# Rounding in ScalarE's affine step, 16-bit transposes of the low halves, and two buffers for two tiles

## The chip, the cores and the metric

The kernel runs on one core of a Trainium2 chip. The metric is the device time of one execution in microseconds (us): the median of three runs of the kernel before is 655.27 us (654.14 to 655.77).

## The reference, cut to what matters

The input `x` is 64 samples of 64 channels by 1024 positions, fp32. Two layers run one after the other:

```python
y  = grouped_conv1d(x, w, taps=9, groups=4) + ctx(cond)[:, :, None] + bias   # L0_cond
# L0_ffn: int8 quantised product
a_scale = max(abs(y), -1) / 127 ; x_q = round(y / a_scale)
w_scale = max(abs(W0), -1) / 127 ; w_q = round(W0 / w_scale)
x  = x + ((x_q @ w_q.T) * a_scale * w_scale).astype(float16)
# L1_cond: a 64x64 mix of the channels per sample, from a small network with softmax
x2 = einsum('boi,bih->boh', agg_w, x) + agg_b[:, :, None]
# L1_ffn: x2 @ W.T + b, plus a rank-32 term gated by a top-2 softmax over 8 experts
x  = x + H + delta
```

## The kernel before, in words

A tile is two samples, that is 128 rows (2 x 64 channels) by 1024 positions; there are NT = 32 tiles. Each engine has its own program, written out by hand, and works it off in order; semaphores (`wait(engine, name, value)` and `.then_inc`) join them. Nothing is planned by a compiler: the order in the text is the order on the engine.

**Before the loop** (about 50 us): the 1024x1024 weight of the first layer is loaded in 8 blocks of 128 rows. VectorE takes each row's maximum (`wq_maxima`), its scale and inverse, and rounds (`wq_round`): times the inverse plus MAGIC. MAGIC is 1.5 x 2^23, so that the fp32 sum has the rounded integer in its low bits. TensorE transposes the blocks as fp32 (`wq_transposed(o, h)`, L421, four 128x128 pieces for each half h into one PSUM bank), and ScalarE writes them as bf16 into `wqT` with bias -MAGIC (`wq_out`, L822). Between these stand the first tiles' steps and the mixing weights: `agg_out` (L831) writes them to `zT`, SyncE stores them to DRAM (L285), loads them back as `mixT` (L290), and then goes on with the loads of the loop, among them `x_ph` for tile 4 and `wst` (L312).

**The loop**, c from 3 to 31. TensorE's order in iteration c is: `conv(c)` (L452), `mix(c-3)` (L495), logits, the first half of `int_product(c-2)` (L511) with `row_total(c-3)` (L475) behind its third matmul, the second half with `max_rows(c)` (L518) inside, `max_back(c)` (L522), `tokens_out(c-1)` (L483), and in odd iterations `rank_pair(c-5)` (L542, L545). The second half of `conv(c)`'s groups waits for `f_ready` of `layer0(c-2, 1)`.

VectorE's order is: `rank_out` in even iterations, `rounded(c-1)` (L1274), `conv_bias(c)` (L1246), `row_max(c)` (L1252), `tile_bound` and `tile_scale` (L1288 to L1295, they give `t_up`), `layer0(c-2, 0)` (L1284), `chan_max(c)`, `low(c-3, 0)` (L1300), `scales(c)` (its last operation gives `yinv`, L1269), `layer0(c-2, 1)`, `low(c-3, 1)`.

ScalarE's order is: `tokens_sb(c-2)` (L845), `row_sums(c-3)` (L840, it gives `x1sum`), `w_abs` in iterations 3 to 10 (L868, from `wst`), `w_high` in 13 to 20 (L878), `w_sums` in 19 to 26 (L873), `high(c-3)` twice (L855), `z_bias` in 4 to 7 (L920), and `scale_rows(c)` (L862).

The path of the tokens of tile t is: `conv_bias` writes `yb` (fp32); `scale_rows` multiplies each of 8 slices by its own inverse scale into `yv` (fp32); `rounded` adds MAGIC and takes it off again, and writes `yq` (bf16); `tokens_out` transposes 8 pieces into PSUM; `tokens_sb` copies them as bf16 into `yqT`; `int_product` multiplies with `wqT`. There is one buffer each of `yb`, `yv`, `yq` and `yqT`. So `conv_bias(t)` waits for `scale_rows(t-1)` (`yv_ready`), and `tokens_sb(t)` for the whole of `int_product(t-1)`. GpSimd adds the residual (`add_layer0`, L1090) and splits weights.

**After the loop** TensorE runs the dense product of the second layer (L574), then 13 pairs of tiles with 7 products each in place of 8 (L768), and the rank term (L750).

## Time and profile before

| | |
|---|---|
| median of three runs | 655.27 us |
| profiled execution: its time | 654.78 us |
| its span, first to last instruction | 653.0 us |
| mean granted clock of TensorE | 0.987 of full speed |
| TensorE busy | 631.6 us (97%) |
| VectorE busy | 435.8 us (67%) |
| ScalarE busy | 337.1 us (52%) |
| GpSimd busy | 336.6 us (52%) |
| share of the chain that ended last | TensorE 75% |

A busy share is an average over stages. The matmuls are pipelined, so a busy TensorE is not one at its peak. "Idle before <-X" in a row is the time for which the engine stood still just before that instruction, and what ended it. In the profile PE is TensorE, PEld its weight loads, DVE VectorE, ACT ScalarE, POOL GpSimd, SP SyncE.

### The profile page before, as it was taken

The page shows a single profiled execution, that of the slowest core. Times are in us where ns is not written, and L with a number is a line of the kernel's source. Part 1 is how long each engine was busy: PE and PEld are TensorE (multiplying, and loading weights), DVE is VectorE, ACT ScalarE, POOL GpSimd, SP SyncE. Part 2 cuts the span into 40 slices and gives each one's busy share as a digit, 9 for nine tenths or more (in the row PEclk, how much of TensorE's full clock was granted, in tenths as well). Part 3 has the DMA queues.
Part 4 walks back from the last instruction along what each step waited for, and adds up shares of the span by engine and source line. Part 5 has one row for each costly group of instructions (what it writes and reads, how often), then busy time and mean ns, then how long its engine had stood idle before and what let it go on. Part 6 is the DMA issues. An engine that isn't in the chain of part 4 may idle for free.

```text
span 653.0 us, 14999 instructions
## 1 busy us (share of the span) xinstructions
PE 631.6 (97%) x5853; PEld 340.6 (52%) x5886; DVE 435.8 (67%) x922; ACT 337.1 (52%) x574; POOL 336.6 (52%) x222
## 2 busy tenths in 40 slices
PE   6998999999999999999999999999999999999997
PEld 4565555556665666665554444444444444444443
DVE  5866887888888888889636697746544333444434
...
GB/s 271 330 132 312 299 296 302 203 243 319 266 288 337 313 347 299 260 213 179 194 132 291 97 34 122 181 222 188 194 193 187 145 123 132 187 194 247 75 1 129
DMA packets 46628, 138.39 MB, mean 212 GB/s; under 512 B 13156, under 2 KB 13444, under 8 KB 46377
## 3 DMA queue, kind: packets, MB, share of 16 engines
...
q14 instruction: 23, 0.19, 0.1%
...
## 4 chain that ended last, share of the span: by engine, by line
PE 75%; DVE 1%; issue 1%; ACT 0%; DVEq 0%; ACTq 0%
PE ps L768 36%; PE ps L511 11%; PE ps L574 9%; PE ps L452 8%; PE ps L495 3%; PE ps L750 2%; PE ps L483 2%; PE ps L542 1%; PE ps L545 1%; PE ps L557 1%; PE ps L522 0%; PE ps L518 0%; ACT yv L862 0%; DVE unscale L1452 0%; DVE z_lo L1311 0%
## 5 line engine op out<-in xcount | busy, mean ns | idle before, releaser
L1090 POOL TENSOR_TENSOR x<-x_in,f_both 128x512 f32<-128x512 f32 x64 | 74.1, 1159 | 201.6 <-DVE f_both L1284 201.6
L511 PE MATMUL ps<-wqT,yq_both 128*128 128x512 bf16 x479 | 113.7, 379 | 6.7 <-issue 4.3
L452 PE MATMUL ps<-x_ph,conv_w 64*64 64x256 f32 (+1 forms) x1024 | 97.2, 392 | 1.6 <-DMA conv_w<-in_conv_taps 1.6
L862 ACT ACTIVATE yv<-yb,yinv 128x128 f32<-128x128 f32 x256 | 78.2, 388 | 26.5 <-DVE yinv L1269 26.3
L901 ACT ACTIVATE ring<-ring,ratio 128x2048 f16<-128x2048 f16 x26 | 50.6, 1994 | 51.0 <-DVE x_ph L1548 14.0
L768 PE MATMUL ps<-ffn_wT,ring 128*128 128x512 f16 x312 | 71.6, 379 | 0.0
L511 PEld LDWEIGHTS ps<-wqT,yq_both 128*128 128x128 bf16 x512 | 45.2, 97 | 49.1 <-ACT yq_both L845 1.5
L452 PEld LDWEIGHTS ps<-x_ph,conv_w 64*64 64x64 f32 (+1 forms) x1024 | 51.1, 137 | 36.6 <-issue 14.4
L855 ACT ACTIVATE ring<-ps,t_up 128x512 f16<-128x512 f32 x64 | 40.5, 684 | 47.0 <-issue 39.4
L574 PE MATMUL ps<-ffn_wT,ring 128*128 128x512 f16 x288 | 64.6, 379 | 0.0
L1121 POOL TENSOR_TENSOR bias_b<-ring 128x1024 f32<-128x1024 f16 x13 | 27.8, 2137 | 48.3 <-ACT ring L901 48.2
L1561 DVE SCALAR_TENSOR_TENSOR x_in<-ps,unscale,x_in 128x512 f32<-128x512 f32 x30 | 22.5, 750 | 43.7 <-PE ps L768 43.5
L1284 DVE SCALAR_TENSOR_TENSOR f_both<-ps,tok_scale,wsc_b 128x512 f16<-128x512 f32 x64 | 47.7, 747 | 4.0 <-PE ps L511 3.9
L768 PEld LDWEIGHTS ps<-ffn_wT,ring 128*128 128x128 f16 x312 | 30.5, 98 | 36.8
L1300 DVE SCALAR_TENSOR_TENSOR ring<-ps,t_up,ring 128x512 f16<-128x512 f32 x64 | 46.9, 736 | 0.8 <-ACT ring L855 0.8
L1246 DVE TENSOR_TENSOR yb<-ps,ybias 128x1024 f32<-128x1024 f32 x32 | 39.0, 1220 | 11.7 <-PE ps L452 8.8
L1561 DVE SCALAR_TENSOR_TENSOR wst<-ps,unscale,wst 128x512 f32<-128x512 f32 x28 | 21.0, 749 | 35.2 <-PE ps L768 35.1
L574 PEld LDWEIGHTS ps<-ffn_wT,ring 128*128 128x128 f16 x288 | 27.2, 98 | 31.8 <-issue 0.8
L1252 DVE TENSOR_REDUCE rowmax<-yb 128x8 f32<-128x1024 f32 x32 | 39.0, 1220 | 1.0
L495 PEld LDWEIGHTS ps<-mixT,x 64*64 64x64 f32 x2048 | 35.5, 135 | 5.0 <-issue 1.3
L1561 DVE SCALAR_TENSOR_TENSOR x<-ps,unscale,x 128x512 f32<-128x512 f32 x21 | 15.8, 750 | 31.1 <-PE ps L768 31.1
L1274 DVE TENSOR_SCALAR yq_both<-yv 128x1024 bf16<-128x1024 f32 x32 | 23.4, 731 | 18.5 <-ACT yv L862 18.5
...
## 6 DMA issues: line engine op xcount, KB each, us to landing
...
```

The source lines that it names most:

```text
L452: return mm(ps_conv[o, g * 2 * MB:(g + 1) * 2 * MB], conv_w[k, g, w.start + o.start:w.start + o.stop], xp[k, g, :, view], start=first, sto ...
L495: last = mm(bank(2 + e)[j * 64:(j + 1) * 64, k * CH:(k + 1) * CH], x1[b, t % 2, l:l + 64], mixT[b, t, b], start=True, stop=True)
L511: last = mm(acc_bank(t, h), yqT[:, p, :], wqT[:, p, h * HALF:(h + 1) * HALF], start=p == 0, stop=p == PH - 1)
L574: last = mm(o, x2_cols[:, x2_slot(n), a, k, :], ffn_wT[:, w, k, h * HALF:(h + 1) * HALF], start=k == 0 and i == 0, stop=k == NL - 1 and i ...
L768: last = mm(b, left(a, k), right(w, k), start=fresh and k == 0 and i == 0, stop=k == 3 and i == 2, skip_group_check=True)
L855: A(x2_cols[:, t % RING, 0, :, h * CH:(h + 1) * CH], bank(2 + h).rearrange("p (c t) -> p c t", c=NL), ACT.Copy, scale=t_up[:, t % 4:t % 4 ...
L862: last = A(yv[:, s, :], yb[:, s, :], ACT.Copy, scale=yinv[:, s:s + 1])
L901: A(cols, cols, ACT.Copy, scale=ratio[:, t:t + 1]).then_inc(sem("norm_ready"), 1)
L1090: g.tensor_tensor(x1[:, t % 2, s], x_in[:, t % 3, s], f16[:, s], ALU.add).then_inc(sem("x1_ready"), 1)
L1284: v.scalar_tensor_tensor(f16[:, s], acc_bank(t, h), tok_scale[:, t % 4:t % 4 + 1], wsc_b[:, s], ALU.mult, ALU.mult).then_inc(sem("f_ready" ...
L1300: v.scalar_tensor_tensor(x2_cols[:, t % RING, 1, :, cols], bank(2 + h).rearrange("p (k t) -> p k t", k=NL), t_up[:, t % 4:t % 4 + 1], x2_c ...
L1561: v.scalar_tensor_tensor(buf, src, unscale[:, t:t + 1], buf, ALU.mult, ALU.add).then_inc(sem("pair_folded"), 1)
```

## The change

- MAGIC grows by 0x6600. The low 16 bits of the fp32 sum are then 0x6600 plus the integer, which read as fp16 is 1536 plus the integer, exactly.
- `scale_rows` adds MAGIC itself: Copy with a scale becomes Identity with a scale and a bias, both read per partition. `rounded` and its buffer are gone; `yq` is a view of `yv`, every second fp16.
- `tokens_out` and `wq_transposed` transpose these fp16 low halves (8 pieces of a weight block into one bank, one eviction); `tokens_sb` and `wq_out` take 1536 off by their bias.
- `yb` and `yqT` have two buffers each; `conv_bias(t)` waits for `scale_rows(t-2)` and `tokens_sb(t)` for `int_product(t-2)`.
- ScalarE runs `tokens_sb(c-1)` in iteration c ahead of `scale_rows(c)`. It ran it in iteration c+1 ahead of `row_sums`.
- `row_total` stands behind the fourth matmul, not the third, and `tokens_out(31)` between the halves of `int_product(30)`.

```diff
--- before.py
+++ after.py
@@ -31,7 +31,8 @@
 NJ = NANCH // P
 ZW = 64 + ZR
 QMAX = 127.0
-MAGIC = 12582912.0
+HALF_BIAS = 1536.0
+MAGIC = 12582912.0 + 0x6600
 EXPMASK = 0x7F800000
 TOP = 13
 RING = 6
@@ -84,11 +85,11 @@
         agg = zT[:, 0:CH * 32].rearrange("b (i o) -> b i o", i=CH)
         x_in = sb("x_in", [P, 3, L], F32)
         x_ph = sb("x_ph", [P, 3, GRP * 2 * MW], F32)
-        yb = sb("yb", [P, 8, MB], F32)
+        yb = sb("yb", [P, 2, 8, MB], F32)
         yv = sb("yv", [P, 8, MB], F32)
         yq_both = sb("yq_both", [P, 2, L], BF16)
-        yq = yq_both[:, 0, :].rearrange("p (s m) -> p s m", s=8)
-        yqT = yq_both[:, 1, :].rearrange("p (s m) -> p s m", s=PH)
+        yq = yv[:, :, :].bitcast(F16).rearrange("p s (m w) -> p s m w", w=2)[:, :, :, 0]
+        yqT = yq_both[:, :, :].rearrange("p a (s m) -> p a s m", s=PH)
         f_both = sb("f_both", [P, 2, L], F16)
         f16 = f_both[:, 0, :]
         abs_junk = f_both[:, 1, :].bitcast(BF16)
@@ -101,6 +102,7 @@
         b_rank = row_bias[0:R, :]
         ident = sb("ident", [P, P], F32)
         identb = sb("identb", [P, P], BF16)
+        identh = sb("identh", [P, P], F16)
         ones16 = sb("ones16", [P, 1], F16)
         ones_b = sb("ones_b", [P, P], BF16)
         conv_w = sb("conv_w", [P, GRP, 16 * CG], F32)
@@ -121,7 +123,8 @@
         att_s = sb("att_s", [B, 4], F32)
         attT = sb("attT", [NK, B], F32)
         set_mask = sb("set_mask", [P, 8], F32)
-        neg_magic = sb("neg_magic", [P, 1], F32)
+        magic = sb("magic", [P, 1], F32)
+        neg_half_bias = sb("neg_half_bias", [P, 1], F32)
         wq_max = sb("wq_max", [P, NL], F32)
         wq_scale = sb("wq_scale", [P, NL], F32)
         wq_inv = sb("wq_inv", [P, NL], F32)
@@ -171,7 +174,7 @@
         gmx = sb("gmx", [P, 8], F32)
         g_top = sb("g_top", [2, 1], F32)
 
-        gate = yb[:, :, :].rearrange("p n (j e) -> p n j e", e=E)
+        gate = yb[:, 0, :, :].rearrange("p n (j e) -> p n j e", e=E)
         top8 = yv[:, 0, :].rearrange("p (j e) -> p j e", e=E)
         gateT = wsc_b[:, 0:P]
 
@@ -181,7 +184,7 @@
             return ps[:, n * 512:(n + k) * 512]
 
         ps_conv, ps_mix, ps_tr, ps_small, ps_dense = bank(0, 2), bank(2, 2), bank(4), bank(5), bank(6, 2)
-        ps_trb = ps_tr.bitcast(BF16)
+        ps_trh = ps_tr.bitcast(F16)
         ps_g = bank(2, 4)
 
         agg_dram = nc.dram_tensor("agg_scratch", [2, B, CH, 32], F32, kind="Internal").ap()
@@ -412,13 +415,14 @@
         def _(pe):
             mm, tr = nc.tensor.matmul, nc.tensor.transpose
 
-            def wq_transposed(o, h):
+            def wq_transposed(o):
                 pe.wait_ge(sem("wq_rounded"), o + 1)
-                if o >= 1:
-                    pe.wait_ge(sem("wqT_ready"), 2 * o - 1 + h)
-                q = wq_nat[:, o * L:(o + 1) * L].rearrange("p (m e) -> p e m", e=PH)
-                for p in range(4):
-                    last = tr(bank(6 + h)[:, p * P:(p + 1) * P], q[:, 4 * h + p, :], ident[:, :])
+                if o == 0:
+                    pe.wait_ge(sem("ident_ready"), 3)
+                wait(pe, "wqT_ready", o - 1)
+                q = wq_nat[:, o * L:(o + 1) * L].bitcast(F16).rearrange("p (m e w) -> p e m w", e=PH, w=2)
+                for e in range(PH):
+                    last = tr(bank(6 + o % 2).bitcast(F16)[:, e * P:(e + 1) * P], q[:, e, :, 0], identh[:, :])
                 last.then_inc(sem("wqT_psum"), 1)
 
             def wq_scales_out(h):
@@ -475,12 +479,12 @@
                 mm(ps_small[:, 140:141], ones_b[:, :], top, start=True, stop=True).then_inc(sem("total_psum"), 1)
 
             def tokens_out(t):
-                wait(pe, "yq_ready", t + 1)
+                wait(pe, "yv_ready", t + 1)
                 wait(pe, "yqT_ready", t)
                 if t == 0:
                     pe.wait_ge(sem("agg_ready"), 4)
                 for s in range(8):
-                    last = tr(ps_trb[:, s * P:(s + 1) * P], yq[:, s, :], identb[:, :])
+                    last = tr(ps_trh[:, s * P:(s + 1) * P], yq[:, s, :], identh[:, :])
                 last.then_inc(sem("yqT_psum"), 1)
 
             def mix(t):
@@ -501,14 +505,14 @@
                     wait(pe, "yqT_ready", t + 1)
                     wait(pe, "f_ready", 2 * t - 1 + h)
                     if t == 0:
-                        pe.wait_ge(sem("wqT_ready"), 8 * h + 8)
+                        pe.wait_ge(sem("wqT_ready"), 4 * h + 4)
                         pe.wait_ge(sem("wsc_ready"), h + 1)
                     elif h == 1:
                         wait(pe, "yb_ready", min(t + 3, NT))
                     if t >= NT - 2:
                         pe.wait_ge(sem("yb_ready"), NT)
                 for p in range(lo, hi):
-                    last = mm(acc_bank(t, h), yqT[:, p, :], wqT[:, p, h * HALF:(h + 1) * HALF], start=p == 0, stop=p == PH - 1)
+                    last = mm(acc_bank(t, h), yqT[:, t % 2, p, :], wqT[:, p, h * HALF:(h + 1) * HALF], start=p == 0, stop=p == PH - 1)
                 if hi == PH:
                     last.then_inc(sem("acc_ready"), 1)
 
@@ -594,40 +598,32 @@
-            wq_transposed(0, 0)
-            wq_transposed(0, 1)
+            wq_transposed(0)
...
@@ -659,9 +655,9 @@
                     wait(pe, "yinv_ready", c)
                     for j in logits_at[c]:
                         logits_out(j)
-                int_product(c - 2, 0, 0, 3)
+                int_product(c - 2, 0, 0, 4)
                 row_total(c - 3)
-                int_product(c - 2, 0, 3, 8)
+                int_product(c - 2, 0, 4, 8)
                 int_product(c - 2, 1, 0, 3)
                 if c == W_BOUND + 1:
                     pe.wait_ge(sem("w_scale_ready"), 2)
@@ -688,8 +684,8 @@
             dense(0, 0, 4, 8)
             row_total(NT - 3)
             int_product(NT - 2, 0)
+            tokens_out(NT - 1)
             int_product(NT - 2, 1)
-            tokens_out(NT - 1)
             dense(0, 1, 0, 5)
             mix(NT - 2)
             int_product(NT - 1, 0)
@@ -817,10 +813,9 @@
             A = nc.scalar.activation
 
             def wq_out(o):
-                for h in range(2):
-                    act.wait_ge(sem("wqT_psum"), 2 * o + h + 1)
-                    A(wqT[:, 4 * h:4 * h + 4, o * P:(o + 1) * P], bank(6 + h).rearrange("p (e c) -> p e c", e=4),
-                      ACT.Identity, bias=neg_magic[:, 0:1]).then_inc(sem("wqT_ready"), 1)
+                act.wait_ge(sem("wqT_psum"), o + 1)
+                A(wqT[:, :, o * P:(o + 1) * P], bank(6 + o % 2).bitcast(F16).rearrange("p (e c) -> p e c", e=PH),
+                  ACT.Identity, bias=neg_half_bias[:, 0:1]).then_inc(sem("wqT_ready"), 1)
 
             def wsc_out(h):
                 act.wait_ge(sem("wsc_psum"), h + 1)
@@ -841,9 +836,9 @@
 
             def tokens_sb(t):
                 wait(act, "yqT_psum", t + 1)
-                wait(act, "acc_ready", 2 * t)
-                A(yqT[:, :, :].rearrange("m p (s c) -> m s p c", s=8),
-                  ps_trb.rearrange("m (s p c) -> m s p c", s=8, p=PH), ACT.Copy).then_inc(sem("yqT_ready"), 1)
+                wait(act, "acc_ready", 2 * (t - 1))
+                A(yqT[:, t % 2, :, :].rearrange("m p (s c) -> m s p c", s=8),
+                  ps_trh.rearrange("m (s p c) -> m s p c", s=8, p=PH), ACT.Identity, bias=neg_half_bias[:, 0:1]).then_inc(sem("yqT_ready"), 1)
 
             def high(t, h):
                 wait(act, "mix_ready", 2 * t + 1 + h)
@@ -857,9 +852,9 @@
 
             def scale_rows(t):
                 wait(act, "yinv_ready", t + 1)
-                wait(act, "yq_ready", t)
+                wait(act, "yqT_psum", t)
                 for s in range(8):
-                    last = A(yv[:, s, :], yb[:, s, :], ACT.Copy, scale=yinv[:, s:s + 1])
+                    last = A(yv[:, s, :], yb[:, t % 2, s, :], ACT.Identity, scale=yinv[:, s:s + 1], bias=magic[:, 0:1])
                 last.then_inc(sem("yv_ready"), 1)
 
             def w_abs(k):
@@ -926,7 +921,7 @@
             A(h1[:, :], bank(2)[:, 64:64 + B], ACT.Gelu, bias=mb01[:, 1:2]).then_inc(sem("h_act"), 1)
             act.wait_ge(sem("att_logits_ready"), 2)
             A(att_e[:, :], att[:, :], ACT.Exp, bias=att_s[:, 0:1]).then_inc(sem("att_exp_ready"), 1)
-            act.wait_ge(sem("ident_ready"), 3)
+            act.wait_ge(sem("ident_ready"), 5)
             wq_out(0)
             act.wait_ge(sem("mlp_psum"), 4)
             A(attT[:, :], bank(2)[0:NK, 192:192 + B], ACT.Copy).then_inc(sem("attT_ready"), 1)
@@ -960,8 +955,6 @@
             A(z_w[:, :, R:ZR], pk[:, PACK["w8"]].rearrange("p (k r) -> p k r", k=NL), ACT.Copy, scale=s_up[:, 0:1]).then_inc(sem("rank_hi_ready"), 1)
 
             for c in range(3, NT):
-                if c > 3:
-                    tokens_sb(c - 2)
                 row_sums(c - 3)
                 if 0 <= c - W_ABS < NL:
                     w_abs(c - W_ABS)
@@ -982,9 +975,9 @@
                     act.wait_ge(sem("b_loaded"), 16)
                     for n in (0, 2):
                         A(b_parts[n * R:(n + 1) * R, :], b_rank, ACT.Copy, scale=s_up[0:R, 3:4]).then_inc(sem("rank_hi_ready"), 1)
+                tokens_sb(c - 1)
                 scale_rows(c)
 
-            tokens_sb(NT - 2)
             t_high(0)
             row_sums(NT - 3)
             high(NT - 3, 0)
@@ -1061,11 +1054,13 @@
             g = nc.gpsimd
             g.memset(ident[:, :], 0.0).then_inc(sem("ident_zero"), 1)
             g.memset(identb[:, :], 0.0).then_inc(sem("ident_zero"), 1)
-            pool.wait_ge(sem("ident_zero"), 2)
-            for m in (ident, identb):
+            g.memset(identh[:, :], 0.0).then_inc(sem("ident_zero"), 1)
+            pool.wait_ge(sem("ident_zero"), 3)
+            for m in (ident, identb, identh):
                 g.affine_select(out=m[:, :], in_=m[:, :], compare_op=ALU.not_equal, fill=1.0, base=0,
                                 pattern=[[-1, P]], channel_multiplier=1).then_inc(sem("ident_ready"), 1)
-            g.memset(neg_magic[:, :], -MAGIC).then_inc(sem("ident_ready"), 1)
+            g.memset(neg_half_bias[:, :], -HALF_BIAS).then_inc(sem("ident_ready"), 1)
+            g.memset(magic[:, :], MAGIC).then_inc(sem("ident_ready"), 1)
 
             def mixT_zero(e):
                 g.memset(mixT[e * CH:(e + 1) * CH, :, (1 - e) * CH:(2 - e) * CH], 0.0).then_inc(sem("mixT_zeroed"), 1)
@@ -1242,14 +1237,14 @@
 
             def conv_bias(t):
                 wait(dve, "conv_ready", t + 1)
-                wait(dve, "yv_ready", t)
-                v.tensor_tensor(yb[:, :, :].rearrange("p (b g) m -> p b g m", b=2), ps_conv.rearrange("p (g b m) -> p b g m", g=GRP, b=2),
+                wait(dve, "yv_ready", t - 1)
+                v.tensor_tensor(yb[:, t % 2, :, :].rearrange("p (b g) m -> p b g m", b=2), ps_conv.rearrange("p (g b m) -> p b g m", g=GRP, b=2),
                                 ybias[:, 2 * t:2 * t + 2, :].unsqueeze(3).to_broadcast([P, 2, GRP, MB]), ALU.add).then_inc(sem("yb_ready"), 1)
 
             def row_max(t):
                 wait(dve, "yb_ready", t + 1)
                 wait(dve, "rowmaxT_ready", t)
-                v.tensor_reduce(rowmax[:, :], yb[:, :, :], AX.X, ALU.max, apply_absolute_value=True).then_inc(sem("rowmax_ready"), 1)
+                v.tensor_reduce(rowmax[:, :], yb[:, t % 2, :, :], AX.X, ALU.max, apply_absolute_value=True).then_inc(sem("rowmax_ready"), 1)
 
             def chan_max(t):
                 wait(dve, "rowmaxT_ready", t + 1)
@@ -1267,12 +1262,6 @@
                 wait(dve, "tok_scale_ready", t + 1)
                 wait(dve, "yv_ready", t)
                 v.reciprocal(yinv[:, :], yscale[:, :]).then_inc(sem("yinv_ready"), 1)
-
-            def rounded(t):
-                wait(dve, "yv_ready", t + 1)
-                wait(dve, "yqT_psum", t)
-                v.tensor_scalar(yq[:, :, :].rearrange("p s m -> p (s m)"), yv[:, :, :].rearrange("p s m -> p (s m)"), MAGIC, -MAGIC,
-                                ALU.add, ALU.add).then_inc(sem("yq_ready"), 1)
 
             def layer0(t, h):
                 wait(dve, "acc_ready", 2 * t + h + 1)
@@ -1376,7 +1365,6 @@
-            rounded(0)
...
@@ -1433,7 +1419,6 @@
                     v.tensor_reduce(w_max[:, :], w_part[:, :], AX.X, ALU.max).then_inc(sem("w_max_ready"), 1)
 
             rank_out(NT - 6)
-            rounded(NT - 1)
             row_scales()
             for t in (NT - 3, NT - 2):
                 tile_bound(t)
```

## Rows read from the trace of the kernel before

**Rows 1.** Busy time by engine in two stretches: stretch, length, busy us (instructions) per engine.

```profile
60.00:100.00 40.00, 38.57 (x585) 24.08 (x592) 33.06 (x82) 35.88 (x75) 10.45 (x9) 1.00 0.80 297
...
209.60:227.70 18.10, 17.78 (x265) 11.13 (x264) 15.78 (x39) 14.55 (x32) 14.55 (x9) 1.00 0.91 336
```

**Rows 2.** Chain that ended last, one round of the steady loop: start us, us, what.

```profile
217.69 2.91 PE ps L452 x32
```

**Rows 3.** Waits of TensorE from 60 to 316 us: total us, times, longest us.

```profile
PE ps L511 <- ACT yq_both L845: 1.7, 2, 1.2
...
PE ps L475 <- ACT f_both L840: 0.6, 3, 0.2
...
PE ps L518 <- DVE bound L1288: 0.6, 1, 0.6
```

**Rows 4.** Timeline of the same steady round: start us, us, engine, line, operation.

```profile
217.07 0.62 PE L483 MATMUL ps<-identb,yq_both 128*128 128x128 bf16 x8
...
217.77 2.44 ACT L862 ACTIVATE yv<-yb,yinv 128x128 f32<-128x128 f32 x8 [0.95 <-DVE yinv L1269]
...
220.12 1.00 ACT L845 ACTIVATE yq_both<-ps 128x1024 bf16<-128x1024 bf16 x1
...
220.24 1.05 DVE L1274 TENSOR_SCALAR yq_both<-yv 128x1024 bf16<-128x1024 f32 x1 [1.18 <-ACT yv L862]
...
221.02 1.04 ACT L840 ACTIVATE f_both<-x 128x1024 bf16<-128x1024 f32 x1
...
221.97 0.19 ACT L840 ACTIVATION_READ_ACCUMULATOR f_both<-x 128x1 f32 x1
...
222.03 0.59 PE L511 MATMUL ps<-wqT,yq_both 128*128 128x512 bf16 x2 [0.16 <-issue]
...
222.49 1.89 PE L511 MATMUL ps<-wqT,yq_both 128*128 128x512 bf16 x8
```

**Rows 5.** ScalarE groups by shape: count, busy us, mean ns, idle before.

```profile
L862 ACT ACTIVATE yv<-yb,yinv 128x128 f32<-128x128 f32 x256 | 78.2, 388 | 26.5 <-DVE yinv L1269 26.3
...
L1005 ACT ACTIVATE yb<-yb 128x128 f32<-128x128 f32 x1 | 0.3, 309 | 1.6 <-DVE yb L1478 1.6
...
L855 ACT ACTIVATE ring<-ps,t_up 128x512 f16<-128x512 f32 x64 | 40.5, 684 | 47.0 <-issue 39.4 <-DVE t_down L1295 4.4 <-PE ps L495 3.1
...
L827 ACT ACTIVATE wsc_b<-ps 128x512 f32<-128x512 f32 x2 | 1.2, 590 | 0.4 <-PE ps L430 0.4
```

**Rows 6.** Start of the loop: one wait of SyncE's queue, then timeline from 48 us.

```profile
SPq L285 <- ACT zT L831: 12.6, 1, 12.6
...
48.38 0.43 SPq L312 DMA_DIRECT2D wst<-in_w_nat  x1
...
50.02 2.98 PE L452 MATMUL ps<-x_ph,conv_w 128*64 128x256 f32 x32
...
56.93 1.06 ACT L868 ACTIVATE f_both<-wst 128x1024 bf16<-128x1024 f32 x1 [2.11 <-DMA wst<-in_w_nat]
...
58.15 1.27 ACT L855 ACTIVATE ring<-ps,t_up 128x512 f16<-128x512 f32 x2
```

**Rows 7.** Timeline before the loop, 22 to 50 us, VectorE, ScalarE and TensorE.

```profile
27.74 1.23 DVE L1246 TENSOR_TENSOR yb<-ps,ybias 128x1024 f32<-128x1024 f32 x1 [2.91 <-ACT yv L862]
...
38.29 1.27 ACT L822 ACTIVATE wqT<-ps,neg_magic 128x512 bf16<-128x512 f32 x2 [0.28 <-PE ps L421]
...
40.40 1.05 PE L421 MATMUL ps<-ident,ffn_wT 128*128 128x128 f32 x8
```

**Rows 8.** Weight loads of fp32 and bf16: duration ns min/median/max.

```profile
L421 PEld LDWEIGHTS ps<-ident,ffn_wT x64: 185/194/231, 15.3 to 41.1; 128*128 128x128 f32 x64
...
L587 PEld LDWEIGHTS ps<-pk x8: 186/192/192, 5.7 to 6.4; 128*128 128x128 f32 x8
...
L483 PEld LDWEIGHTS ps<-identb,yq_both x256: 95/98/147, 33.2 to 328.6; 128*128 128x128 bf16 x128
```

**Rows 9.** One microsecond early on; the number after the engines is the granted clock.

```profile
8.00:9.00 1.00, 0.38 (x2) 0.29 (x2) 1.00 (x4) 0.98 (x2) 0.00 (x0) 0.52 1.07 426
```

23 lines of the change are left out of this document (7 added, 16 removed).

## The prediction

> **What bounds the kernel now.** I read four views: the busy time by stretch, the chain that ended last, the waits of TensorE, and the timeline of one steady round. In a steady round of the loop TensorE is busy for 17.78 of 18.10 us, two iterations [rows 1]; the chain through it (one piece in [rows 2]) consists of TensorE pieces alone. All that TensorE lost to others between 60 and 316 us is small: 1.7 us to the eviction of the transposed tokens, 0.6 us to the row sums, 0.6 us to VectorE [rows 3]. So work taken from VectorE gives little by itself, and work added to ScalarE costs little only as long as ScalarE stays in time. ScalarE is close: 35.88 of 40 us busy from 60 to 100, 14.55 of 18.10 in the steady round [rows 1].
>
> The step to watch is `row_total`, a matmul inside `int_product` that waits for `x1sum` (`row_sums`, L840). ScalarE works in order, and `row_sums` stands behind `scale_rows` and `tokens_sb`. In the steady round `scale_rows` starts at 217.77, `tokens_sb` at 220.12, `row_sums` at 221.02, and its accumulator read ends at 222.16 [rows 4]. TensorE goes on past `row_total` at 222.49. The slack is 0.33 us, less about 0.10 us from accumulator read to matmul.
>
> **The change, part by part.**
>
> *`rounded` goes (VectorE).* 32 x 0.73 us; in the steady round it ran 220.24 to 221.29, drawn out by its wait for ScalarE [rows 4]. TensorE hides nearly all of it already. What it gives is the 0.6 us of L518 behind VectorE's bound [rows 3], and about as much in the same crowded iteration by a late `chan_max` and `layer0`: -1.0.
>
> *`scale_rows` does the rounding (ScalarE).* Before, one L862 operation reads one per-partition pointer, the scale. Afterwards it reads two, scale and bias. No operation of this trace has both, so the second is bounded. Below: 0, if both are fetched together; a gain is excluded, as nothing is taken from the operation. Above: what the first pointer costs. That is 388 - 309 = 79 ns for 128x128 and 684 - 590 = 94 ns for 128x512 [rows 5]. Both pairs differ in more than the pointer (function, source or output type). I take 90 ns: operations follow each other every 2.35 / 8 = 294 ns (217.77 to 220.12), and I expect every 384 ns: 8 x 0.09 = +0.72 us a tile. `tokens_sb` gets its first pointer, +0.09.
>
> The Trainium skill, page "ScalarE: Activation LUTs", section "What ACT_TABLE_LOAD costs", speaks against this edit: each per-partition pointer operand adds about 93 ns, over an operation with immediate scale and bias. The trace agrees for one pointer; no row has two. By 93 ns a tile would pay 0.74 us, by none 0.
>
> *`tokens_sb(c-1)` moves from behind `scale_rows(c)` to ahead of it.* It waits for `tokens_out(c-1)`, whose eight transposes end at 217.07 + 0.62 = 217.69; today `scale_rows` starts at 217.77, held by yinv [rows 4]. Behind the waiting `tokens_sb` are `scale_rows` and then `row_sums`. `tokens_sb` starts at 217.73 and takes 0.90 + 0.09 to the next start, so `scale_rows` starts at 218.72 and `row_sums` at 218.72 + 8 x 0.384 = 221.79. Its accumulator read ends 1.14 later (222.16 - 221.02), at 222.93, and TensorE can go on at 223.03. Nothing else moves: the evicted tokens are now early, so the 1.7 us of L511 [rows 3] go, but in those iterations `row_sums` is as late as before and takes most of the wait over; I keep -0.4.
>
> *`int_product` split after 4 instead of 3 matmuls.* `row_total` comes one matmul (0.22) later, at 222.71. Stall: 223.03 - 222.71 = 0.32 us. In the other iteration of the pair the 16 matmuls of `rank_pair` stand between the transposes and the next convolution and cover it. The loop has 10 such pairs from iteration 13 on: 10 x 0.32 = +3.2. With 79 ns: 9 x 11 ns less, 0.22 each, +2.2.
>
> *Iterations 4 to 12.* ScalarE also has `w_abs` and `z_bias` there. 40 us hold 4.4 iterations; 35.88 + 4.4 x 0.81 = 39.4 of 40 us. It still fits in sum, but the waits for `t_up` between have no room. Ends: 0, or all 9 x 0.81 = 7.3 on TensorE. I take +2.0, nearer the lower end.
>
> *Second buffers for `yb` and `yqT`.* `conv_bias` no longer waits for the tile before; in the steady round its convolution is what it waits for anyway. 0.
>
> *First weight.* Eight fp32 transposes took 1.05 us, eight 16-bit ones take 0.62 [rows 4, 7]; two evictions of 1.27 us together become one of about 1.0 + 0.09. Over eight blocks 3.4 us of TensorE and some 1.5 us of ScalarE. With `conv_bias(1)` freed of its 2.91 us wait [rows 7], I get the third convolution of the loop's start (conv(3), at 50.02 [rows 6]) 3 to 4 us earlier. But that is taken back at once: `w_abs(0)` waits for `wst`, issued at 48.38 and started on at 56.93, and `high(0)` follows at 58.15; `layer0(1,1)`, for which conv(4) waits, stands behind it on VectorE. These transfers hang on the chain of the mixing weights, whose first store waits for ScalarE's L831 [rows 6], and there `scale_rows(0)` is 0.72 longer and `wq_out(2)` 0.2 shorter: +0.5 for the transfer, against 0.5 that a freed VectorE gains behind `high(0)`. Net 0. Bounds: -0.5 to +0.5.
>
> *Strided fp16 weight loads.* The transposes now load weights two elements apart (sixteen for the first weight). No 16-bit load here is strided; fp32 ones are: 194 ns at a step of eight elements against 192 ns contiguous [rows 8]. So 0; the upper end is the fp32 price, 194 against 98 ns [rows 8].
>
> *Identity, memsets, end of the loop.* A third identity is two more GpSimd operations while TensorE waits for its first data; `tokens_out(NT-1)` is moved between two products, where its input has long been ready. 0, up to 0.3.
>
> **Sum.** -1.0 - 0.4 + 3.2 + 2.0 + 0 + 0.2 = +4.0 us on the profiled execution's 654.78 (span 653.0), 658.8; the median shown is 0.5 above it: 659.3 us. Own range 657.0 to 662.5.
>
> **The rivals.**
>
> *B, faster: the second pointer is (nearly) free.* Place: the eight operations of L862. `row_sums` must start by 222.71 - 0.10 - 1.14 = 221.47; it starts at 220.98 + 9p, so the stall begins at p = 54 ns. Below that the 3.2 and 2.0 go, what ScalarE had as waits remains, and -1.4 stands, with another 0.5 from the start and 0.5 from the later `row_total`: -2.4, 652.9 us. For: no row shows two pointers. Against: every row with one pays.
>
> *C, nothing to see: the price is paid and hidden.* p near 60 ns gives a stall of 0.05 a pair, and the first iterations balance -1.4: 655.3 us.
>
> *D: strided 16-bit loads run at the fp32 rate.* Eight transposes would take 1.05 instead of 0.62 [rows 4, 7]: 32 x 0.43 = +13.8 on top, 673 us. Against: rows 8. The Trainium skill, "SBUF — State Buffer", section "Door 1: The DMA port swizzle", has steps within 16 bytes free, which would hold for the tokens; for the first weight's 32 bytes it names a penalty, which the fp32 loads at that step don't show.
>
> *E: TensorE's clock falls at the loop's start.* With the start 3 us earlier and conv(4) where it was, TensorE stands nearly idle before 60 us. Early on the granted clock was 0.52 (the 1.2 GHz level) in a microsecond in which TensorE had been busy for 0.38 us [rows 9]. Three us of work at the lower level cost +1.5 on A: 661 us.
>
> *That the change doesn't do what it says* I exclude: all three edits are in the diff as described.
>
> **How the numbers follow.** A 0.45, B 0.31, C 0.14, D 0.04, E 0.06. The likeliest is A. The range reaches to B and E: 652.3 to 662.5; D and the rest lie outside. About 0.3%, 2.0 us, is what a measurement of this kernel can tell from none: faster (below 653.3) has most of B, 0.25; same (653.3 to 657.2) has what is left of B, a part of C and the low end of A, 0.22; slower has the rest, 0.53.
>
> **What would show it.** L862's successor at 460 to 480 ns instead of 388, `row_sums` starting some 0.8 us later after the transposes, and waits of TensorE's L475 <- ACT of some 0.3 us in every second iteration (0.6 us in all before). conv(3) at 46 to 47 us and conv(5) hardly moved. L483's successor unchanged at 98 ns. Wrong if L862's successor stays under 440 ns, or if conv(5) too is 3 us earlier.

## The result, and the profile after

The changed kernel took 659.17 us (median of 13 runs, 656.39 to 663.03); the kernel before, on the same chip, 655.0 us (13 runs, 653.42 to 655.9). The ratio is 1.0062, 95% interval 1.0044 to 1.0081: slower, by some 4 us. Forecast were 659.3 us and a chance of 0.53 for slower. The profiled execution took 657.43 us (span 655.6), 1.7 us below its median; that gap is taken up below.

Lines have shifted: `conv` is L456 (before L452), `int_product` L515 (L511), `row_total` L479 (L475), `tokens_out` L487 (L483), `scale_rows` L857 (L862), `tokens_sb` L840 (L845), `row_sums` L835 (L840), `w_abs` L863 (L868), `high` L850 (L855), `conv_bias` L1241 (L1246), `layer0` L1273.

Groups of ScalarE in the changed kernel, by shape (count, busy us, mean ns, idle before):

```profile
L857 ACT ACTIVATE yv<-yb,magic,yinv 128x128 f32<-128x128 f32 x256 | 101.6, 482 | 1.6 <-DVE yinv L1264 1.6
...
L840 ACT ACTIVATE yq_both<-ps,neg_half_bias 128x1024 bf16<-128x1024 f16 x32 | 35.6, 1113 | 29.9 <-PE ps L487 29.5
```

The `in` side of L857 now names two pointers, `magic` and `yinv`, and one operation takes 482 ns instead of the 388 of [rows 5]: 94 ns more. L840 has its first pointer.

Busy time by stretch, as in [rows 1]: the crowded 40 us, and one steady pair of rounds, which now has 18.44 us:

```profile
60.00:100.00 40.00, 38.35 (x608) 23.28 (x607) 30.30 (x73) 37.84 (x72) 9.47 (x9) 1.00 0.81 298
209.96:228.40 18.44, 18.26 (x270) 11.06 (x267) 14.77 (x37) 16.11 (x32) 14.76 (x9) 1.00 0.86 311
```

VectorE (the third figure) has lost work and ScalarE (the fourth) has gained it; of the 40 us ScalarE now fills 37.84. TensorE is a little less busy in the first of them, and its pair is 0.34 us longer.

Waits of TensorE from 60 to 320 us (total us, times, longest us):

```profile
PE ps L479 <- ACT f_both L835: 5.1, 12, 1.8
PE ps L673 <- DVE yinv L1264: 0.5, 1, 0.5
PE ps L526 <- DVE chanmax_rep L1253: 0.2, 1, 0.2
```

The two waits for the evicted tokens and for VectorE's bound in [rows 3] are gone, as predicted; in their place stand twelve waits at `row_total` for `x1sum`. One steady round shows how each comes about (start us, us, engine, line, operation; the bracket is idle time and its releaser):

```profile
217.59 0.62 PE L487 MATMUL ps<-identh,yv 128*128 128x128 f16 x8
...
218.25 1.11 ACT L840 ACTIVATE yq_both<-ps,neg_half_bias 128x1024 bf16<-128x1024 f16 x1 [0.91 <-PE ps L487]
...
219.27 3.17 ACT L857 ACTIVATE yv<-yb,magic,yinv 128x128 f32<-128x128 f32 x8
...
222.32 1.04 PE L515 MATMUL ps<-wqT,yq_both 128*128 128x512 bf16 x4
222.35 1.04 ACT L835 ACTIVATE f_both<-x 128x1024 bf16<-128x1024 f32 x1
...
223.29 0.19 ACT L835 ACTIVATION_READ_ACCUMULATOR f_both<-x 128x1 f32 x1
223.53 0.10 PEld L479 LDWEIGHTS ps<-x1sum,ones_b 128*128 128x128 bf16 x1 [0.67 <-ACT f_both L835]
223.53 0.18 PE L479 MATMUL ps<-x1sum,ones_b 128*128 128x1 bf16 x1 [0.18 <-ACT f_both L835]
...
223.57 1.67 PE L515 MATMUL ps<-wqT,yq_both 128*128 128x512 bf16 x7
```

Read it from the transposes down. ScalarE starts on the tokens as soon as they are out, goes through `scale_rows` in 3.17 us instead of 2.44 [rows 4], and comes to `row_sums` 4.76 us after the transposes began; before it was 221.02 - 217.07 = 3.95 us. That is 0.81 us later, TensorE has four matmuls to do meanwhile, and then it waits. The next product matmuls follow 223.57 - 222.32 = 1.25 us after the first four began. In the round before this one, where `rank_pair` covered ScalarE, it was 0.90 us. The difference is 0.35 us. The waits view counts only 0.18 of it. Part of the rest is that the weight load of L479 can no longer run ahead: in the round before it began 0.21 us ahead of its matmul (214.41 against 214.62), here both begin at 223.53.

What each stretch cost is best seen from the starts of `conv(t)` on TensorE. The table has the start in the kernel before, and how many us later (+) or earlier (-) the same convolution starts in the other kernels. Three profiles of the changed kernel were taken; the experiments in the table are described below.

```
                         conv(3)  conv(4)  conv(5)  conv(13)  conv(31)   span
before                    50.02    60.30    68.60    144.42    308.40   653.0
changed                   -2.80    -2.68    -2.21     -0.60     +2.29   655.6
changed, second profile   -3.97    -3.84    -3.26     +0.04     +2.92   656.2
changed, third profile    -3.19    -3.05    -1.20     +0.41     +3.29   656.6
e1 one pointer            -5.71    -5.80    -4.38     -5.32     -5.30   648.0
e3 row_total 6            -4.45    -4.32    -2.97     -2.89     -2.84   650.4
e4 before + pointer       +0.61    +1.35    +2.04     +5.05     +9.97   663.6
e5 weight only            -2.93    -2.93    -2.31     -2.11     -2.12   650.8
e6 one yb                 -0.36    -0.96    +0.71     +1.21     +1.54   654.8
e9 total 6 to 12          -2.69    -2.55    -2.00     -1.90     +0.99   654.3
e10 total 6 from 13       -2.82    -2.68    -1.96     -0.34     -0.32   653.0
```

So the changed kernel gains 1.2 to 3.3 us before conv(5), loses 1.6 to 3.3 up to conv(13), loses 2.9 in the steady pairs, the same in all three profiles, and 0.3 behind them. How far one execution differs from another before the loop can be read from six profiles of kernels that are alike up to there (changed three times, e3, e9, e10): conv(3) starts between 45.57 and 47.33 us. A difference of 1.8 us at conv(3) between single profiles is therefore not an edit's worth; the distances from conv(13) to conv(31) agree to 0.01 us in the three profiles of the changed kernel.

The start, in the timeline of the changed kernel:

```profile
47.22 2.98 PE L456 MATMUL ps<-x_ph,conv_w 128*64 128x256 f32 x32
...
47.44 0.43 SPq L315 DMA_DIRECT2D wst<-in_w_nat  x1
...
55.33 1.06 ACT L863 ACTIVATE f_both<-wst 128x1024 bf16<-128x1024 f32 x1 [2.57 <-DMA wst<-in_w_nat]
...
56.39 1.25 ACT L850 ACTIVATE ring<-ps,t_up 128x512 f16<-128x512 f32 x2
...
59.02 2.11 PE L456 MATMUL ps<-x_ph,conv_w 128*64 128x256 f32 x24 [0.24 <-DVE f_both L1273]
```

Against [rows 6] the convolution is 2.80 us earlier, but so are `wst`'s issue, by 0.94, and `w_abs(0)`, by 1.60 us. The last row is the cost of the chain that the prediction named: conv(4) stops inside, until `layer0(1,1)` is done. In the kernel before it ran through:

```profile
60.39 2.95 PE L452 MATMUL ps<-x_ph,conv_w 128*64 128x256 f32 x31
```

### The profile page after: what moved, and what is told of

Same layout as the page of the kernel before. It is cut to its first block, busy times and chain, and to the rows that moved or that the text cites. A ratio compares the mean times of both kernels' runs of the same rounds, so it can differ in the third digit from the quotient of the medians.

```text
span 655.6 us, 14956 instructions
## 1 busy us (share of the span) xinstructions
PE 635.5 (97%) x5886; PEld 337.6 (51%) x5886; DVE 419.5 (64%) x890; ACT 360.6 (55%) x566; POOL 336.6 (51%) x225
## 4 chain that ended last, share of the span: by engine, by line
PE 50%; DVE 1%; issue 0%; ACT 0%; DVEq 0%
PE ps L764 36%; PE ps L578 9%; PE ps L746 2%; PE ps L515 2%; PE ps L499 1%; PE ps L456 0%; PE ps L546 0%; DVE unscale L1437 0%; DVE z_lo L1300 0%; DVE ring L1289 0%; DVE zT L1302 0%; PE ps L549 0%; PE ps L724 0%; PE ps L487 0%; DVE x_ph L1331 0%
## 5 line engine op out<-in xcount | busy, mean ns | idle before, releaser
L515 PE MATMUL ps<-wqT,yq_both 128*128 128x512 bf16 x512 | 122.8, 381 | 0.0
L857 ACT ACTIVATE yv<-yb,magic,yinv 128x128 f32<-128x128 f32 x256 | 101.6, 482 | 1.6 <-DVE yinv L1264 1.6
L456 PE MATMUL ps<-x_ph,conv_w 64*64 64x256 f32 (+1 forms) x1024 | 98.2, 394 | 1.4 <-DMA conv_w<-in_conv_taps 1.0
L456 PEld LDWEIGHTS ps<-x_ph,conv_w 64*64 64x64 f32 (+1 forms) x1024 | 50.9, 137 | 37.2 <-issue 14.4
L515 PEld LDWEIGHTS ps<-wqT,yq_both 128*128 128x128 bf16 x512 | 45.3, 98 | 46.2 <-issue 1.1
L1241 DVE TENSOR_TENSOR yb<-ps,ybias 128x1024 f32<-128x1024 f32 x32 | 39.1, 1223 | 40.9 <-PE ps L456 29.2
L850 ACT ACTIVATE ring<-ps,t_up 128x512 f16<-128x512 f32 x64 | 40.4, 681 | 26.9 <-issue 21.7
L1273 DVE SCALAR_TENSOR_TENSOR f_both<-ps,tok_scale,wsc_b 128x512 f16<-128x512 f32 x64 | 47.8, 748 | 7.2 <-PE ps L515 6.6
L840 ACT ACTIVATE yq_both<-ps,neg_half_bias 128x1024 bf16<-128x1024 f16 x32 | 35.6, 1113 | 29.9 <-PE ps L487 29.5
```

The source lines that it names most:

```text
L456: return mm(ps_conv[o, g * 2 * MB:(g + 1) * 2 * MB], conv_w[k, g, w.start + o.start:w.start + o.stop], xp[k, g, :, view], start=first, sto ...
L515: last = mm(acc_bank(t, h), yqT[:, t % 2, p, :], wqT[:, p, h * HALF:(h + 1) * HALF], start=p == 0, stop=p == PH - 1)
L850: A(x2_cols[:, t % RING, 0, :, h * CH:(h + 1) * CH], bank(2 + h).rearrange("p (c t) -> p c t", c=NL), ACT.Copy, scale=t_up[:, t % 4:t % 4 ...
L857: last = A(yv[:, s, :], yb[:, t % 2, s, :], ACT.Identity, scale=yinv[:, s:s + 1], bias=magic[:, 0:1])
L1273: v.scalar_tensor_tensor(f16[:, s], acc_bank(t, h), tok_scale[:, t % 4:t % 4 + 1], wsc_b[:, s], ALU.mult, ALU.mult).then_inc(sem("f_ready" ...
```

## The experiments

The experiments ran later, on three chips, where the kernel before took 654.30 to 654.36 us, some 0.65 us less than beside the changed kernel above. Where a time is set against the 659.17 us of the changed kernel, that much of the distance is not the edit's; the ratios are free of it.

**Is it the second pointer? e1, e2.** `magic` is one value for all partitions, so the bias need not be a pointer.

```
-  A(yv[:, s, :], yb[:, t % 2, s, :], ACT.Identity, scale=yinv[:, s:s + 1], bias=magic[:, 0:1])
+  A(yv[:, s, :], yb[:, t % 2, s, :], ACT.Copy, scale=yinv[:, s:s + 1], bias=MAGIC)
```

> The changed kernel with scale_rows as Copy with the scale read per partition and MAGIC as an immediate bias: one pointer instead of two, the same sum. Theory (second pointer): scale_rows falls from 482 to about 388 ns an operation, row_sums is again in time for row_total, TensorE's waits for x1sum fall from 5.1 us to under 1 us in all, a steady pair of iterations takes 18.1 instead of 18.45 us, and the time is 652.5 us (651 to 654.5), some 0.4% under the kernel before. Rival (the loss comes from the strided fp16 loads, the order on ScalarE or the two buffers): the time stays at 657 to 661 us, and the waits stay whatever scale_rows takes.

Measured: 652.45 us (12 runs, 649.77 to 654.84), ratio to before 0.9968 (0.9951 to 0.9985). Its row of L857 and its waits of TensorE from 60 to 320 us:

```profile
L857 ACT ACTIVATE yv<-yb,yinv 128x128 f32<-128x128 f32 x256 | 77.9, 389 | 1.6 <-DVE yinv L1264 1.6
```

```profile
PE ps L479 <- ACT f_both L835: 1.4, 2, 1.1
```

The operation is back at 389 ns, a steady pair takes 18.09 us as before, and the kernel is 6.7 us under the changed one (some 6 us by the ratios) and faster than the one before. Its waits fell to 1.4 us, not under the 1 us expected. The three edits together are worth having; the pointer turned them into a loss. e2 gives `tokens_sb` and `wq_out` an immediate bias too, in the same way (`ACT.Copy, bias=-HALF_BIAS`).

> As e1, and the two evictions (tokens, first weight) too take their -1536 as an immediate with Copy. Theory: 0.09 us less per tile on ScalarE for tokens_sb and 0.7 us less before the loop; 652.2 us (650.5 to 654), at most 0.5 us under e1, since after e1 ScalarE is in time. Rival (any work on ScalarE counts on the path): 32 x 0.09 = 2.9 us under e1.

Measured: 651.69 us (650.07 to 653.82), ratio 0.996 (0.9944 to 0.9977). L840 fell from 1113 to 1021 ns: the same price for the same thing. By the time, e1 and e2 can't be told apart.

**Is it the place of `row_total`? e3.** The pointers stay, and TensorE gets two more matmuls to do before it waits.

```
-  int_product(c - 2, 0, 0, 4)
+  int_product(c - 2, 0, 0, 6)
   row_total(c - 3)
-  int_product(c - 2, 0, 4, 8)
+  int_product(c - 2, 0, 6, 8)
```

> The changed kernel with row_total behind the sixth matmul of the product instead of the fourth, both pointers kept. Theory (the loss is the wait at row_total): it stands 0.43 us later, the steady stall of 0.35 us goes, the pair takes 18.1 us; the stalls of the crowded first iterations (1.06, 0.48, 1.8 us) lose 0.43 each. 3 to 4.5 us under the changed kernel: 655.5 us (654 to 657). Rival (ScalarE's load as such: the delay is only handed on to t_up, high and low, for which the next mix waits): 658 to 660 us, with the same sum of waits at another instruction.

Measured: 653.47 us (651.85 to 659.73), ratio 0.9994 (0.9973 to 1.0014), under the 654 to 657 us expected. L857 is still at 482 ns; the waits of TensorE from 60 to 320 us are

```profile
PE ps L479 <- ACT f_both L835: 2.0, 2, 1.4
```

ScalarE has as much work as in the changed kernel, and the time is 5.7 us shorter (some 4.5 by the ratios). From conv(3) to the end, where alone the edit acts, its profile is 3.5 to 5.3 us shorter than the three of the changed kernel. It is not the added work that costs, then, but that TensorE comes to `row_total` before it is done.

**The pointer without the rest: e4.** The kernel before, with a pointer to a column of zeros as second operand.

```
-  A(yv[:, s, :], yb[:, s, :], ACT.Copy, scale=yinv[:, s:s + 1])
+  A(yv[:, s, :], yb[:, s, :], ACT.Identity, scale=yinv[:, s:s + 1], bias=zero[:, 0:1])
```

> The kernel before with one thing changed: scale_rows is Identity with a second pointer, to a column of zeros. Theory: 482 ns instead of 388, row_sums 0.75 us later against a slack of 0.23 us: a stall of 0.5 us in every steady pair (10 pairs, +5 us), and 2 to 4 us in iterations 4 to 12, where VectorE's rounded and conv_bias also wait for scale_rows: 662 us (659 to 666). Rival (a second pointer costs nothing by itself, the loss is in the rest of the change): 655 us.

Measured: 665.46 us (4 runs, 664.96 to 665.69), ratio 1.0169 (1.015 to 1.0188). The operation and TensorE's waits from 60 to 320 us:

```profile
L863 ACT ACTIVATE yv<-yb,zero,yinv 128x128 f32<-128x128 f32 x256 | 101.9, 480 | 25.3 <-DVE yinv L1271 25.1
```

```profile
PE ps L512 <- ACT yq_both L846: 4.0, 5, 1.7
PE ps L476 <- ACT f_both L841: 2.8, 13, 0.2
```

The price is 92 ns, nearly the same, so it doesn't hang on what the other edits do. Here the pointer costs 11 us, more than twice what the whole change does: `tokens_sb` still stands behind `scale_rows`, so the tokens are late as well, and TensorE waits in two places.

**Where does the gain at the start come from? e5, e6.** e5 is the kernel before with the first weight's edit alone (`wq_transposed`, `wq_out` and their waits as in the diff).

> The kernel before with one of the three edits alone: the first weight's rounded sums transposed as fp16 halves (eight 16-bit transposes and one eviction a block instead of eight fp32 ones and two). ScalarE's scale_rows, VectorE's rounded and all buffers are those of before. Theory (what the changed kernel gains before the loop comes from the weight blocks and is kept): conv(3) 1.5 to 3 us earlier than before, the difference carried unchanged to conv(31), a median of 652 to 653.7 us. Rival 1 (the second yb buffer gives the start, by freeing conv_bias(1)): conv(3) within 0.5 us of before, 654.5 to 655.5 us. Rival 2 (as the prediction had it, given back at once to transfers of wst): conv(3) 2 to 3 us earlier, conv(5) within 0.5 of before, 654.5 to 655.5 us.

Measured: 653.1 us (11 runs, 651.1 to 657.55), ratio 0.9985 (0.997 to 1.0001). conv(3) is 2.93 us earlier, conv(5) 2.31 and conv(31) still 2.12: some 0.8 us are lost on the way, the rest is kept to the end. Rival 1 wanted conv(3) unmoved and rival 2 conv(5); neither is so. These are one profile against one, and the medians differ by 1.2 us only; the time itself can't be told from no change with certainty. e6 is e1 with one `yb` buffer, so that `conv_bias` waits again for the tile before:

```
-  wait(dve, "yv_ready", t - 1)
-  v.tensor_tensor(yb[:, t % 2, :, :]...
+  wait(dve, "yv_ready", t)
+  v.tensor_tensor(yb[:, 0, :, :]...
```

> The changed kernel with the immediate bias in scale_rows (as in e1_imm_rows, 652.45 us) and one yb buffer again: conv_bias(t) waits for scale_rows(t-1). yqT keeps its two buffers. Theory (second yb buffer matters only before the loop, where conv_bias(1) waited 2.9 us in the kernel before): that wait is back at 2 to 3 us, conv(3) at 45 to 47 us instead of 44.6, no difference added after conv(5), 653 to 654.5 us. Rival (the buffer gives nothing anywhere, since chan_max or the weight blocks are what the start waits for): 652 to 652.9 us. Rival (it matters in every iteration, since conv_bias comes before scale_rows in time): conv starts lose 0.1 us or more per pair, over 655 us.

Measured: 653.66 us (12 runs, 652.1 to 656.6), ratio 0.9987 (0.9974 to 0.9999). The wait at conv_bias(1) is back, and conv_bias(1) starts at 30.03 us; with two buffers it started at 25.10 in the changed kernel.

```profile
30.03 1.23 DVE L1241 TENSOR_TENSOR yb<-ps,ybias 128x1024 f32<-128x1024 f32 x1 [2.83 <-ACT yv L857]
```

The medians differ by 1.2 us from e1's, but the intervals overlap, and the profiled executions are the slowest of one kernel and the fastest of the other, so their 5 us at conv(3) are not the buffer's worth. In the loop more can be read. There VectorE's waits from 50 to 320 us have this first line in e6, and no such line in e1:

```profile
DVE yb L1241 <- ACT yv L857: 30.9, 14, 3.5
```

From conv(5) to conv(31) e6 loses 0.8 us against the kernel before, 0.3 of it behind conv(13) at 0.04 us a pair, where e1 gains 0.9. So the second buffer of `yb` is worth something in the loop too, 1.7 us in these profiles, most of it in the crowded iterations up to conv(13); the expectation had nothing behind conv(5). By the medians alone its worth is not settled.

**Do the cures add up? e7.** The biases of e2 with the split of e3.

> Both cures together: immediate biases on all of scale_rows, tokens_sb and wq_out (as e2_imm_all, 651.69 us), and row_total behind the sixth matmul of int_product (as e3_row_total_6, 653.47 us). Theory (both remove the same stall, so they don't add up): the remaining 1.4 us of TensorE's waits for x1sum fall to under 0.5, steady pair 18.09 us as with either, 650.5 to 651.7 us. Rival (each removes its own loss: 6.7 and 5.7 us below the changed kernel): 646 to 648 us.

Measured: 650.51 us (12 runs, 649.34 to 655.86), ratio 0.9962 (0.9943 to 0.9982). TensorE's waits at `row_total` from 60 to 320 us:

```profile
PE ps L479 <- ACT f_both L835: 0.6, 1, 0.6
```

They don't add up: the remaining wait is a little over the half microsecond expected, and the time is that of e2 within its uncertainty. Both remove one stall. It is the lowest median here, 8.7 us below the changed kernel's and 3.8 below the one of the kernel before beside it, and it beats both kernels.

**What of the spread? e8.** The changed kernel again.

> The changed kernel again, unchanged, for a second profile beside the first (span 655.6 us; conv(3) at 47.22, conv(13) at 143.82, conv(31) at 306.9 or so) and more runs: its times spread over 6.6 us where those of before spread over 2.5. Theory (the spread comes from the first 145 us, where ScalarE has no room and the start's transfers and clock vary; from conv(13) on each pair costs 18.44 us in every execution): conv(31) minus conv(13) equal to the first profile's within 0.3 us, and whatever the spans differ by is there by conv(13). Rival (the steady part varies too, as the stall depends on VectorE's and the DMA's times): conv(31) minus conv(13) differs by over 0.5 us. Median 658 to 660 us.

Measured: 658.18 us (6 runs, 656.21 to 660.61), ratio 1.0057 (1.0041 to 1.0074). conv(31) minus conv(13) is 166.86 us against 166.87: the steady part does not vary. conv(13) minus conv(5) does: 79.12 us against 77.43. All of that arises in one place. The longest wait at `row_total`, in the changed kernel's first profile:

```profile
110.82 0.18 PE L479 MATMUL ps<-x1sum,ones_b 128*128 128x1 bf16 x1 [1.83 <-ACT f_both L835]
110.86 1.67 PE L515 MATMUL ps<-wqT,yq_both 128*128 128x512 bf16 x7
```

and in its second:

```profile
109.76 0.18 PE L479 MATMUL ps<-x1sum,ones_b 128*128 128x1 bf16 x1 [1.83 <-ACT f_both L835]
109.80 2.77 PE L515 MATMUL ps<-wqT,yq_both 128*128 128x512 bf16 x7
```

Ahead of it in ScalarE's line stand the two copies of the second bias (first profile):

```profile
103.21 2.31 ACT L977 ACTIVATE b_parts<-row_bias,s_up 32x1024 f16<-32x1024 f32 x2
```

The wait is the same to the hundredth, but the seven matmuls behind it take 2.77 us instead of 1.67. The second profile by stretches shows why (stretch, length, busy us of PE, PEld, DVE, ACT and POOL, then the granted clock, DMA share, GB/s):

```profile
108.00:110.00 2.00, 0.24 (x2) 0.14 (x3) 0.60 (x2) 1.91 (x5) 0.00 (x0) 1.00 1.01 290
110.00:112.00 2.00, 2.00 (x7) 0.74 (x6) 1.24 (x5) 2.00 (x4) 0.00 (x0) 0.55 1.01 367
112.00:114.00 2.00, 2.00 (x8) 0.76 (x6) 1.22 (x4) 0.10 (x1) 1.15 (x1) 0.59 0.58 236
```

TensorE was busy for 0.24 of 2 us, and behind that the granted clock stood at about half, the 1.2 GHz level. In the first profile, with the same wait, it stayed at 1.00. A stall can be paid twice; that it was the stall which brought the clock down is argued from the order of the two, no run shows it apart.

**The two stretches apart: e9, e10.** The edit of e3 in iterations 3 to 12 only, and from 13 on only (`n0 = 6 if c <= 12 else 4`, and `c >= 13`).

> The changed kernel with row_total behind the sixth matmul of int_product in iterations 3 to 12 only; from 13 on behind the fourth, as changed. It measures the prediction's term for iterations 4 to 12 by itself. Theory (those iterations cost the changed kernel 1.6 to 3.3 us by waits at row_total, the longest of 1.83 us, and more where TensorE's clock falls behind that wait, as it did at 110 to 114 us in the second profile): conv(13) minus conv(5) falls from 77.4 (79.1 in the second profile) to about 75.9, steady pair still 18.44 us, median 656 to 657 us. Rival (the steady pairs alone carry the loss, the early waits only move elsewhere): 658 us or more.

Measured: 656.16 us (11 runs, 655.3 to 659.25), ratio 1.0032 (1.002 to 1.0045). conv(13) minus conv(5) is 75.92 us, and the steady pairs still lose 2.89 us.

> The changed kernel with row_total behind the sixth matmul from iteration 13 on only. It measures the ten steady pairs by themselves. Theory: steady pair 18.09 us instead of 18.44, so conv(31) minus conv(13) falls from 166.87 to 164.0, iterations 5 to 12 as in the changed kernel, median 655.5 to 656.3 us (2.9 less than the changed kernel's 658.2 to 659.2). Rival (the row_total moved later makes the bound late on VectorE and with it the next high(t)): pair over 18.2 us and 657 us or more.

Measured: 654.99 us (11 runs, 654.02 to 656.88), ratio 1.0017 (1.0007 to 1.0027), half a microsecond under what was expected. conv(31) minus conv(13) is 164.00 us, conv(13) minus conv(5) 77.44. Each edit takes its own stretch's loss and leaves the other's alone; the two terms of the sum are separate.

**Two more profiles: e11, e12.** The changed kernel, and e1's.

> The changed kernel once more, for a third profile of it. Theory (what its executions differ in after 60 us is whether TensorE's granted clock falls behind its longest wait at row_total, 1.83 us near 110 us): either the granted clock is 1.00 throughout 38 to 640 us and conv(13) minus conv(5) is 77.4, or it falls near 110 us and the difference is 79.1. Rival (other causes): a difference between those two, or over 79.5, without a low granted clock there.

Measured: 658.38 and 661.04 us. Above 38 us the granted clock was 1.00, and conv(13) minus conv(5) was 77.43, as the theory had it. But the clock is not all that differs: between conv(4) and conv(5) this execution lost 1.85 us, most of it inside conv(4):

```profile
60.03 2.11 PE L456 MATMUL ps<-x_ph,conv_w 128*64 128x256 f32 x24 [1.62 <-DVE f_both L1273]
```

> The kernel of e1_imm_rows once more, for a second profile: the first was the fastest of its twelve executions (649.77 against a median of 652.45 us). Theory (its executions too differ by where the granted clock is low before the loop, and by what the start then takes): conv(3) 1 us or more later than the 44.57 of the first profile, from conv(5) on the same distances as there, within 0.3 us to conv(31). Rival (the difference arises later): conv(3) within 0.3 us of 44.57 and a later loss.

Measured: 652.16 us (4 runs, 650.48 to 654.52). The theory failed: in e1 conv(3) starts at 44.31 us (the 44.57 of the expectation is its third matmul), and here at 44.92, 0.6 us later and not 1 us. Most of the difference came behind it, in conv(4) again:

```profile
54.31 1.06 ACT L863 ACTIVATE f_both<-wst 128x1024 bf16<-128x1024 f32 x1 [4.58 <-DMA wst<-in_w_nat]
...
57.99 3.43 PE L456 MATMUL ps<-x_ph,conv_w 128*64 128x256 f32 x24 [2.24 <-DVE f_both L1273]
```

TensorE waits 2.24 us, and its 24 matmuls take 3.43 us instead of 2.11, while the granted clock fell (columns as above):

```profile
56.00:58.00 2.00, 0.01 (x1) 0.01 (x1) 1.85 (x7) 2.00 (x5) 0.00 (x0) 1.00 1.03 421
58.00:60.00 2.00, 2.00 (x16) 0.92 (x20) 0.60 (x1) 2.00 (x8) 1.16 (x1) 0.63 0.80 324
60.00:62.00 2.00, 2.00 (x49) 1.45 (x44) 0.51 (x1) 1.71 (x3) 0.00 (x0) 0.52 1.05 410
```

The profile of e2 has the longest wait at this place, without a fall of the clock:

```profile
58.63 2.11 PE L456 MATMUL ps<-x_ph,conv_w 128*64 128x256 f32 x24 [2.85 <-DVE f_both L1273]
```

In both kernels conv(4) begins 5.7 us earlier than before, and by conv(5) 3.1 (e2) and 4.1 us (e12, 1.3 of them by slower matmuls) of it are gone; in e1 it was 1.4 of 5.8. So there is a giving back behind `wst`, as the prediction had it, but in no profile of the changed kernel, of e1, e2 or e12 does it take the whole gain.

## Why the prediction was right, and where not

The forecast (A) hit the median within 0.2 us (all 21 executions of the changed kernel, those of e8 and e11 included, have a median of 658.5 us), and the mechanism that gives it its sign held. Its sum was made on the profiled execution, though, and there it came to +4.0 us where three profiles of the changed kernel show +2.6, +3.2 and +3.6. Going through it:

- **`scale_rows`, second pointer: right.** 90 ns taken, 94 measured (92 in e4). The bound from the nearest rows with one pointer and none was nearly the whole answer. The Trainium skill ("ScalarE: Activation LUTs", "What ACT_TABLE_LOAD costs") states 93 ns for each pointer operand; the trace of the changed kernel agrees for a second pointer beside a first.
- **Steady pairs: right.** +3.2 forecast, +2.89 measured: `row_sums` 0.81 us later (0.8 forecast), and 0.35 us a pair (0.32), but in eight pairs rather than ten. e10 takes this term away and nothing else. The view of waits shows half of the stall; judged by it, the term would look too large.
- **Iterations 4 to 12, VectorE's and the tokens' gains: mis-sized.** The three terms (+2.0, -1.0, -0.4) made +0.6. Measured are +1.6 in two profiles and +3.3 in the one where the clock fell behind the stall. The waits that were to go went, but the stalls at `row_total` came in their place, one of 1.83 us: `w_abs`, `high`, `z_bias` and the two copies of the second bias stand in line with `scale_rows` there, and "it still fits in sum" says nothing of one iteration. e9 shows the term's cause: with `row_total` two matmuls later the stretch takes 75.92 us instead of 77.43. Without the second pointer the same stretch gains 0.9 us (e1) and 1.3 (e12), which is what the two forecast gains were worth (1.4 forecast), the second buffer of `yb` included; the pointer's price there was then 1.6 + 0.9 = 2.5 us or a little more where 2.0 was taken, and 4.2 with the clock's fall.
- **Second buffers in the loop: put at 0, not shown to be 0.** The prediction looked at the steady round alone. With one `yb` (e6) the stretch from conv(5) to conv(13) takes 1.4 us more than in e1, and the steady pairs 0.3 us in all.
- **The start: the step that failed.** The prediction had conv(3) at 46 to 47 us, which came (47.22, 46.05, 46.83), and had it all taken back by conv(5), "Net 0. Bounds: -0.5 to +0.5". Kept were 2.2, 3.3 and 1.2 us. The chain was seen rightly, and the three profiles show its place: conv(4) waits inside for `layer0(1,1)`, 0.24, 0.35 and 1.62 us. But `wst` was not held where it was: it was issued 0.3 to 1.8 us earlier, and `w_abs(0)` started 0.6 to 2.7 us earlier. By the prediction's own words it would be "wrong if conv(5) too is 3 us earlier"; it was 1.2 to 3.3. e5 shows whose gain it can be: with the weight blocks alone conv(3) is 2.9 us earlier in its profile, of which 2.1 reach the end (1.2 by the medians), so their size stays open by about a microsecond. That e5 and the changed kernel have conv(3) at the same time fits with the second buffer of `yb` paying for what three `scale_rows` before the loop take more; this is argued, not shown.
- **The errors partly cancel.** Start -2 instead of 0, middle +1.6 and more instead of +0.6, and the profiled execution 1.7 us below its median where 0.5 was allowed. The median was met more closely than the sum deserves.
- **B's time was right, its condition false, its sum not the measured one.** Take the pointer away, and the time is what B said: 652.9 forecast, 652.45 measured (e1). So p was indeed the number on which faster or slower hung. But B had 0.5 us from the start, where e1 and e12 have 4.4 and 1.6 at conv(5), and 0.5 from the later `row_total`, where the steady pairs gain nothing (164.00 us from conv(13) to conv(31) against 163.98). C, a price of some 60 ns that is hidden, is out by the 94 ns.
- **D: refuted for the tokens.** The tokens' loads, two elements apart, take what those of before did. For the first weight, sixteen elements apart, there is a price. The weight loads of the changed kernel (duration min/median/max in ns):

```profile
L487 PEld LDWEIGHTS ps<-identh,yv x256: 96/98/151, 30.9 to 329.5; 128*128 128x128 f16 x128
```

```profile
L425 PEld LDWEIGHTS ps<-identh,ffn_wT x24: 143/148/171, 15.9 to 24.1; 128*128 128x128 f16 x24
```

  The second row is from 15 to 26 us, at a granted clock of 1.00. 98 against 148 ns, so the prediction was wrong to let the fp32 loads at that step [rows 8] stand for 16-bit ones. The Trainium skill ("SBUF — State Buffer", "Door 1: The DMA port swizzle") has steps within 16 bytes free and a price beyond, and this trace agrees with both, for 16-bit loads; the fp32 loads at the larger step [rows 8] show no price. It costs little, for 64 loads only: eight transposes took about 0.72 us, not 0.62.
- **E: not as stated, but its kind occurs.** No profile of the changed kernel has the clock low between 38 and 60 us; e1 (45 to 48 us) and e12 (58 to 62) have. And in the second profile of the changed kernel it fell at 110 us, a place the prediction did not think of, at 1.7 us.

Open stays how the spread of 6.6 us divides. Three places are shown: the start up to conv(3) (1.8 us in the six profiles), the wait inside conv(4) (up to 1.4 us between the three of the changed kernel), and the clock behind the stall at 110 us (1.7 us, in one of the three). What decides in an execution whether the clock falls behind the same 1.83 us of wait, and when `wst` lands, no run tells.
